# An attention and FFN kernel on one core: another place in the step for the high halves, the low halves and the shift of x

## The reference

```python
def _L0_xattn_ref(q, k, v, Wq, Wk, Wv, Wo):          # k = v = ctx, 16 heads of 32
    q = jnp.einsum('bsd,de->bse', q, Wq)
    k = jnp.einsum('bsd,de->bse', k, Wk)
    v = jnp.einsum('bsd,de->bse', v, Wv)
    qh, kh, vh = (_split(q), _split(k), _split(v))
    qh, kh = (_rope(qh), _rope(kh))
    score = jnp.einsum('bhqd,bhkd->bhqk', qh, kh) * scale
    attn = jax.nn.softmax(score, axis=-1)
    out = jnp.einsum('bhqk,bhkd->bhqd', attn, vh)
    ...
    return jnp.einsum('bsd,de->bse', out, Wo)

def _L0_ffn_ref(x, w_gate, w_up, w_down):            # act_qdq: levels by one largest value of the tensor
    x = act_qdq(x)
    up = act_qdq(x @ lpbq_dequant(w_up).T)
    gate = act_qdq(x @ lpbq_dequant(w_gate).T)
    sig = fixed_qdq_u16(jax.nn.sigmoid(gate))
    gate = act_qdq(gate * sig)
    o = act_qdq(gate * up)
    return o @ lpbq_dequant(w_down).T

x = x + _L0_xattn_ref(_layernorm(x, axis=-1), ctx_1024, ctx_1024, Wq, Wk, Wv, Wo)
x = x + _L0_ffn_ref(_layernorm(x, axis=-1), w_gate, w_up, w_down)
```

## Time and profile before

| what | before |
|---|---|
| median of 3 runs | 2343.86 us (2343.57 to 2348.62) |
| profiled execution | 2340.16 us |
| span of the profile | 2338.3 us |
| mean granted clock of TensorE | 0.977 |
| TensorE busy | 2209.0 us (94%) |
| VectorE busy | 1675.0 us (72%) |
| ScalarE busy | 1325.5 us (57%) |
| POOL busy | 695.5 us (30%) |

### The profile page before, as it was taken

One profiled execution on the slowest core, in us unless ns is written; L12 is line 12 of the kernel. 1 busy time (PEld: TensorE's weight loads), 2 busy tenths in 40 slices (PEclk: granted clock), 3 DMA queues, 4 the chain that ended last, 5 costly groups with the idle time before them and its releaser, 6 DMA issues. The chain is left out here.

```text
span 2338.3 us, 31144 instructions
## 1 busy us (share of the span) xinstructions
PE 2209.0 (94%) x12037; PEld 973.0 (42%) x12037; DVE 1675.0 (72%) x1703; ACT 1325.5 (57%) x1299; POOL 695.5 (30%) x655
## 2 busy tenths in 40 slices
PE   5898999899997899999999999999999699999999
PEld 3443333333332444444444444444444244444444
DVE  7546878888876857545543498888888887777773
ACT  3345655656554232322322687787787677777772
POOL 4354565656644401000100164444444000000000
PEclk8899999999998999999999999999999899999999
DMA  6333676776787477788876798787777466655552
GB/s 194 91 103 110 175 170 174 168 184 163 194 163 176 141 214 252 252 247 258 264 231 198 254 352 308 281 299 285 280 282 290 164 234 233 233 209 207 212 218 90
DMA packets 286711, 500.14 MB, mean 214 GB/s; under 512 B 187500, under 2 KB 189804, under 8 KB 249692
## 3 DMA queue, kind: packets, MB, share of 16 engines
q1 hardware_dynamic: 286556, 498.09, 67.2%
HBM read 247.75 MB, written 186.58 MB: 186 GB/s over the span
## 5 line engine op out<-in xcount | busy, mean ns | idle before, releaser
L1684 PE MATMUL banks<-XB,W 128*128 128x512 f16 x2304 | 500.1, 380 | 2.3 <-ACT XB L1710 2.3
L1684 PE MATMUL banks<-XB,WT 128*128 128x512 f16 x2304 | 497.4, 379 | 0.0
L2150 PE MATMUL banks<-W,OH 128*128 128x512 f16 x2256 | 487.1, 379 | 3.6 <-DVE OH L2252 3.6
L1704 ACT ACTIVATE OB<-banks,uns 128x512 f32<-128x512 f32 x384 | 255.6, 683 | 393.9 <-PE banks L1684 391.1
L1684 PEld LDWEIGHTS banks<-XB,W 128*128 128x128 f16 x2304 | 225.9, 98 | 276.1 <-issue 5.0
L1684 PEld LDWEIGHTS banks<-XB,WT 128*128 128x128 f16 x2304 | 225.4, 98 | 271.8
L2150 PEld LDWEIGHTS banks<-W,OH 128*128 128x128 f16 x2256 | 220.7, 98 | 270.0 <-DVE OH L2252 4.1
L1971 POOL TENSOR_TENSOR PR<-GS,OB 128x2048 f32<-128x2048 f32 x46 | 220.5, 4793 | 257.6 <-ACT OB L1704 247.6
L1793 DVE TENSOR_REDUCE amx<-OB 128x1 f32<-128x2048 f32 x48 | 109.7, 2286 | 239.7 <-ACT OB L1704 239.7
L741 PE MATMUL banks<-XC,AH 128*128 128x512 f16 x768 | 190.5, 402 | 4.2 <-POOL AH L1496 3.6
L966 ACT ACTIVATE P<-banks 120x2048 f32<-120x2048 f32 x60 | 112.4, 1873 | 127.5 <-PE banks L664 127.5
(11 more groups left out here) (271 smaller groups left out, 2881.6 us busy)
## 6 DMA issues: line engine op xcount, KB each, us to landing
g_s<-OB SPq DMA_DIRECT2D x48, 1024.0 KB, 6.0
GL<-g_s SPq DMA_DIRECT2D x48, 1024.0 KB, 7.4
up_s<-OB SPq DMA_DIRECT2D x48, 1024.0 KB, 4.9
XA<-up_s SPq DMA_DIRECT2D x32, 1024.0 KB, 9.4
gq_s<-GQ SPq DMA_DIRECT2D x48, 512.0 KB, 4.9
XD<-gq_s SPq DMA_DIRECT2D x48, 512.0 KB, 6.7
XA<-in_x SPq DMA_DIRECT2D x16, 1024.0 KB, 6.4
QW<-QE SPq DMA_DIRECT2D x128, 128.0 KB, 2.5
```

The lines of the kernel that those rows point to most:

```text
L1684: t = e.matmul(pk[:].rearrange("p (j t) -> p j t", j=4), WT[w][:, ot, wa, kk, :], XB[i % 2][:, xa, :, kk, :], start=(kk == 0 and wa == 0 a ...
L1704: e.activation(OB[n % 3][:, r, :], bank[(k + 4) % 8][:], ACT.Copy, scale=uns[:, 12 * w + ot:12 * w + ot + 1]).then_inc(s_ev, 1)
L2150: t = e.matmul(pk[:].rearrange("p (r n) -> p r n", r=4), OH[i % 2][:, a, ot, j * 128:(j + 1) * 128], WD[:, :, c, wa, o4, :], start=(ot == ...
```

## The change

For the batches whose step is 16 or later, three calls move within the body of a step:

- `act_x_high` moves from the head of ScalarE's step to behind the exponents, the copies of values and queries, and the half-precision copies.
- `dve_x_low` moves from ahead of the largest scores to behind them, and behind the aggregate of x1 (`dve_x1_aggregate`).
- `dve_x_shift` moves from behind the largest scores to ahead of them.

```diff
--- before.py
+++ after.py
@@ -954,8 +954,6 @@
             for s in range(NSTEP):
                 b, c = divmod(s, 4)
                 kv = list(kv_at(s))
-                for nb in x_at(s, 2) if s >= 16 else []:
-                    act_x_high(e, nb)
                 u = s - 7
                 if 0 <= u < NU:
                     e.wait_ge(s_c1, u + 1)
@@ -987,6 +985,8 @@
                     e.activation(QE[n % 2][:], BQ_, ACT.Copy, scale=qsc[:]).then_inc(s_qe, 1)
                 if HALF <= s - 1 < NU:
                     act_half(e, s - 1)
+                for nb in x_at(s, 2) if s >= 16 else []:
+                    act_x_high(e, nb)
                 if s == 1:
                     act_split(e, 2)
                     act_ctx(e, 1)
@@ -1311,8 +1311,9 @@
                 if c == 0 and 0 <= b - 3 < B:
                     dve_recip(e, b - 3)
 
-                for nb in x_at(s, 2) if s >= 16 else []:
-                    dve_x_low(e, nb)
+
+                for nb in x_at(s, 1) if s >= 16 else []:
+                    dve_x_shift(e, nb)
                 if s in (11, 12):
                     dve_amax(e, {11: 7, 12: 8}[s])
 
@@ -1359,9 +1360,9 @@
                 for ob in deviations_at(s):
                     dve_x1_aggregate(e, ob)
 
-                for nb in x_at(s, 1):
+                for nb in x_at(s, 1) if s < 16 else []:
                     dve_x_shift(e, nb)
-                for nb in [1] if s == 2 else x_at(s, 2) if s < 16 else []:
+                for nb in [1] if s == 2 else x_at(s, 2):
                     dve_x_low(e, nb)
                 for nb in x_at(s, 0):
                     dve_x_stats(e, nb)
```

## The result

| what | before | after |
|---|---|---|
| median of 5 runs each, same chip | 2343.86 us (2342.65 to 2348.62) | 2330.52 us (2325.63 to 2332.34) |
| ratio, 95% interval | | 0.9934 [0.9917, 0.9950] |
| profiled execution | 2340.16 us | 2325.63 us |
| span | 2338.3 us | 2323.8 us |
| mean granted clock | 0.977 | 0.985 |

The change gains 13.3 us by the medians and 14.5 us between the two profiled executions. I forecast 5.1: the direction holds, and the measured time lies in the stated range of 2325 to 2350 us, but the size is off by a factor of 2.6 to 2.8. The gain is also larger than the 10.6 us that the forecast's own bounds allowed; the range takes it in only because it was stretched towards the rival of the vanished stall.

What follows compares the result with a forecast made beforehand. TensorE's stall for the exponents and a nearly equal second loop through SyncE's transpose; 10.3 + 17.0 + 11.6 + 0.15 = 39.05 against 39.46 us, ten periods 4.1 plus stage's end 1.0, -5.1 us: 2338.8 us, range 2325 to 2350 us.

Steps and rivals of the forecast that it cites:

- the rival of the vanished stall: TensorE's wait for the exponents goes and SyncE's queue doesn't matter: gain 39.7 us, 2304.2 us; chance 0.10.
- Part 1: VectorE's shift ahead of largest scores: normals start some 2.0 us earlier, largest scores end later, +0.15 us per period.
- Part 2: ScalarE's exponents ahead of the high halves: start at P + 1.4; TensorE's 2.85 us stall and slow clock go.
- Part 3: VectorE's largest scores ahead of the low halves: low halves start at P + 7.0, end at P + 10.5.
- Part 4: Transpose in SyncE's queue: starts at P + 10.3 instead of P + 10.71, not before P + 10.0.
- as the rival had it: VectorE's low halves and POOL's multiplication meet every time: gain used up, -1 to +2 us, 2343.9 us; chance 0.20.
- The sum's second term: Second loop, from the transpose to the largest scores two steps on: 17.0 us, the mean of 11.
- less than 15 us after the transpose: Sign against the 17.0 us: largest scores two steps on coming sooner than 15 us after the transpose.
- Third term: Second loop, from the largest scores to TensorE's scores: 11.6 us, plus 0.15 for the shift.
- The stage's end: End of the attention stage: the last transpose starts 10.3 instead of 11.26 us after its scores, gaining 1.0 us.
- The new stall: TensorE's scores (L657) wait for the largest scores, about 2.5 us per period, in place of L705's wait.
- slow clock: Rival: 1.2 GHz after the wait ahead of step 32 costs TensorE 1.70 us there: 2349.8 us; chance 0.18.

Runs made afterwards that it cites:

- run 10: Changed kernel with the transpose ahead of the two transfers of reciprocals in SyncE's queue; 2394.2 us, ratio 1.0235.
- run 8: Changed kernel with four buffers instead of two for the spread reciprocals, so the transpose is issued earlier; 2329.85 us, ratio 0.9950.
- run 9: Changed kernel with SyncE waiting for POOL's second multiplication ahead of both transfers of reciprocals, the swap staying early; 2349.86 us, ratio 1.0040.
- run 1: Kernel before the change with only the shift moved ahead of the largest scores; 2325.67 us, ratio 0.9932.
- run 12: Changed kernel with VectorE's reciprocals computed earlier, ahead of x1's range; 2326.24 us, ratio 0.9945.
- run 6: As the study counts its time: changed kernel with the transposes from batch 5 on replaced by plain copies of the same bytes; 2307.87 us.
- run 7: Changed kernel with one more copy of 256 KB in SyncE's queue ahead of each of the 11 transposes; 2335.21 us, ratio 0.9976.
- run 4: Changed kernel with the shift left behind the largest scores, where it was before; 2327.21 us, ratio 0.9934.

## Why the prediction was right in direction and too small

**What sets SyncE's release.** In one period of each kernel, from its timeline, in us behind the start P of the scores: when the pair of reciprocal transfers could run (the later of its issue and the landing of the second transfer of the pair before, seen as the start of POOL's second multiplication), when the transpose was issued, and when SyncE was free:

| kernel, scores at | pair can run | transpose | free | from "can run" to free |
|---|---|---|---|---|
| before, 367.97 | 9.39 (issue) | 10.71 | 19.07 | 9.68 |
| after, 406.86 | 8.88 (landing) | 11.08 | 18.17 | 9.29 |
| shift alone, 366.22 | 8.14 (landing) | 10.14 | 17.46 | 9.32 |
| exponents alone, 377.02 | 7.98 (landing) | 10.36 | 17.09 | 9.11 |
| all but the shift, 367.86 | 7.92 (landing) | 11.36 | 18.04 | 10.12 |
| low halves alone, 373.98 | 9.53 (issue) | 14.13 | 19.69 | 10.16 |
| four buffers, 367.85 | 8.86 (landing) | 9.26 | 18.40 | 9.54 |
| reciprocals late, 371.90 | 10.39 (issue) | 11.71 | 20.68 | 10.29 |
| reciprocals computed early, 368.26 | 8.19 (landing) | 11.09 | 17.56 | 9.37 |
| more bytes, 367.90 | 8.77 (landing) | 11.72 | 19.14 | 10.37 |

In the first nine rows the last column stays within 9.1 to 10.3 us while the transpose starts anywhere from P + 9.3 to P + 14.1. Over all eleven periods of these nine kernels it lies between 9.1 and 10.6, while the hold goes from 5.4 to 9.3. The last row has 256 KB more in the queue; its mean is 10.4 where the changed kernel's is 9.5. The hold is a remainder: what the queue of transfers still has to do, two of 256 KB and the transpose itself.

The order within the queue can be read from the packets. First the changed kernel and the one before, each in a stretch in which the transpose was issued (417.94, 378.68) and the pair still under way, then each near the end of the hold:

```profile
DMA packets 124, 0.25 MB, mean 98 GB/s; under 512 B 4, under 2 KB 4, under 8 KB 124
...
DMA packets 121, 0.24 MB, mean 80 GB/s; under 512 B 4, under 2 KB 4, under 8 KB 121
...
DMA packets 1701, 0.44 MB, mean 290 GB/s; under 512 B 1701, under 2 KB 1701, under 8 KB 1701
...
DMA packets 2833, 0.73 MB, mean 290 GB/s; under 512 B 2833, under 2 KB 2833, under 8 KB 2833
```

(The stretches are 420.0 to 422.5 and 381.0 to 384.0, then 423.5 to 425.0 and 385.5 to 388.0.) Small packets alone move in the hold of run 10, where only the transpose is in flight (216 GB/s from 399.5 to 403.0), so they are the transpose's. Behind the pair some 400 of them move soon after the issue (419 packets under 512 B from 417.94 to 422.6), and the bulk only when the pair is through; it takes some 3 us. In run 8, where the transpose is issued at 377.11, its bulk comes from 384.0 on as well. While only the pair moves, the DMA engines are busy to a share of 0.26 (420.0 to 422.5): as much as four of the sixteen. Two transfers of 256 KB at 98 GB/s take an estimated 5.3 us. POOL's waits show a similar pace, one transfer landing some 3.2 us behind the other (412.51 and 415.74 above).

Before, the pair went out at P + 9.4, behind the swap, while its predecessors had landed at P + 8.0 (375.96 in the earlier trace rows): 1.4 us in which nothing of this chain ran. The swap was late because its queries are copied behind L705, which the stall of 2.85 us held. The same stall that I took away from TensorE's loop thus stood in SyncE's loop as well. As means of eleven the pair could run at P + 9.18 before and at P + 8.44 after, and SyncE was free at P + 18.99 and P + 17.96: 0.74 of the 1.03 us is the earlier start, and what shortened the rest by 0.29 us stays open. Run 8 moves the transpose and not the pair, run 9 the pair and not the swap; the release follows the pair.

**Point by point.**

- *Part 1, shift: +0.15 us.* True for what it adds, but I left to part 2 what it does alone (run 1). I priced the normals' earlier start at nothing, though the numbers were at hand: 2.0 of a stall of 2.85 us, and the slow clock with it.
- *Part 2, exponents at P + 1.4, stall and slow clock gone:* right, P + 1.39 or 1.40 in all periods. The wait of L705 didn't fall under 3 us in total, my sign of being right, but to 8.9 us. A new short one, 0.67 us, stands a step later, where the exponents follow a second high half of A (L1005, 417.26) that waits for POOL's multiplication of 415.74.
- *Part 3, low halves from P + 7.0:* right, P + 6.88.
- *Part 4, transpose at P + 10.3:* it came at P + 11.03 in the mean. I let POOL's second multiplication end at P + 9.3, its old place and length. Now it starts at P + 8.2 to 9.05 under the low halves, which end at P + 9.24, and ends at P + 10.36 or 10.37 in ten of the eleven periods, 1.1 us behind them whatever its own start: 1.49 us long when it starts at 415.74, 2.16 at 528.58 (P + 8.21), against 1.27 before. So the low halves and POOL do meet nearly every time, as the rival had it, and the side that pays is POOL. By the Trainium skill, SBUF — State Buffer, section "Who interferes with whom", such a pair contends, and who issues first makes the other wait; the rows agree, for here the low halves issue first. In run 12, where POOL starts 0.53 us into them, both are longer (3.40 and 1.79), as in step 29 before. The rival's time, 2343.9, followed from this term alone and was wrong with it, since the start of the transpose doesn't set the release (run 8).
- *The sum's second term, 17.0:* this is the step that failed. I took the hold as a property of the transpose and carried the mean of this term over from the kernel before. It measured 15.31 us, 1.55 less per period than the 16.86 before. The rows that should have warned me are in the prediction itself: 15.7 to 18.1 is no constant. My own test, "less than 15 us after the transpose", was also badly set: the two terms only mean something as a sum, and 10.3 + 17.0 = 27.3 became 26.34, and these 0.96 us in ten periods are what the forecast misses.
- *Third term, 11.6 + 0.15:* 11.77, right.
- *The stage's end, 1.0 us:* it measured 3.7. The eleventh period's stall had little of a second loop behind it, which I hadn't counted: its first step takes 8.85 us (633.89 to 642.74) instead of 13.46 (645.01 to 658.47), 4.6 less, of which 3.7 are left at the end; not tried by itself.
- *The new stall, 2.5 us at L657 per period:* there, but 13.3 us in 18 pieces, up to 2.1, where I expected some ten of 1.5 to 3.

Of the rivals, *the stall is simply gone* (2304.2) fell: run 6 gets near it, 2307.87, only by taking away the hold. The *slow clock* ahead of step 32 didn't come: the granted clock is 1.00 from 246.2 to 693.2, with waits of up to 2.1 us. My reason, that the new stall is shorter than 2.85 us, doesn't carry that, and part of it is luck. In other runs waits as short were followed by 1.2 GHz, as in run 7:

```profile
672.60 1.13 PE L659 MATMUL banks<-QR,KR 32*120 32x512 f32 x8 [2.02 <-DVE MX L1330]
...
673.80:677.10 3.30, 3.30 (x12) 1.19 (x9) 2.71 (x6) 2.37 (x2) 0.89 (x1) 0.50 0.45 105
```

So were waits of 1.90 and 1.88 us in run 9 (484.14 and 645.61, clock 0.50 from 485.7 and from 646.1), while one of 3.19 us in run 4 (692.25) and two of 2.94 and 2.99 in the kernel before (415.33 and 613.16) were not. The length of the wait alone doesn't tell what the clock will do. The loss that the rival describes is part of what run 9 measured.

## What to carry to other kernels

When a stall in one loop is removed, follow what the stalled engine would have fed: here the same 2.85 us also delayed a swap and two transfers in another queue, and the second loop, taken as fixed, shrank by three times what I had counted for it (1.35 us per period, not 0.41). The duration of a queue entry that waits for its predecessors isn't its own (4.82 us with nothing ahead, up to 9.3 behind the pair); add from the moment its predecessors can start, and not from its issue. And before several moves are made at once, look for the smallest one: 0.15 us of shift ahead of a reduction of 2.15 us gave 0.9932, and two of the other moves, each by itself, 1.0081 and 1.0042. Four versions, the changed kernel, the shift alone, all but the shift and the reciprocals computed early, have ratios of 0.9932 to 0.9945 with intervals that overlap; none is clearly the best.

## What was not expected of the hardware

- The transpose in SyncE's queue held it for 4.82 us with nothing ahead, 7.09 behind two transfers of reciprocals, 9.14 when issued sooner behind the same two.
- A transfer of 256 KB that reads 8 KB and writes each row to 32 partitions lands about 3.2 us behind the one before it, some 80 GB/s, and such transfers go one after another. While only they move, all sixteen DMA engines together are busy to 0.26 at 98 GB/s. That it reads four rows may be why; it wasn't tried with more.
- Waits of TensorE of 1.88 to 2.19 us were followed by 1.2 GHz in runs 7 and 9, others of up to 3.30 us were not (run 12, 691.08).
- VectorE's low halves and POOL's multiplication, overlapping: 2.36 (for both) and 1.32 to 2.16 us when POOL comes near their end, 3.40 and 1.79 when it comes near their start; alone 1.22 each and 1.27.
